# A decoder of four layers on one Trainium2 core: head sums through DRAM by batch, and the output projection inside the score steps

## The reference, cut to what matters

```
q, k, v   = projections of layernorm(x) and of the context (or of x)
num[b,h]  = exp(q k^T / sqrt(8) - rowmax) v          # 8 values per head and query
den[b,h]  = sum of the same exp over the keys
attn      = num / den                                 # in the gated one den >= 1e-30, and * sigmoid(xn Wg + bg)
x        += attn Wo + bo
```

## Time and profile before

| | us |
|---|---|
| time, median of 3 runs (1762.51 to 1765.19) | 1764.23 |
| the profiled execution, its own time | 1759.35 |
| its span, first to last instruction | 1757.6 |
| PE busy over the span | 1491.2 (85%) |
| DVE busy | 1012.8 (58%) |
| ACT busy | 797.9 (45%) |
| POOL busy | 449.6 (26%) |
| mean granted TensorE clock | 0.917 |
| hardware DMA queue, share of 16 engines | 15.3% |

### The profile page before, as it was taken

One profiled execution on the slowest core, in us unless ns is written; L12 is line 12 of the kernel. 1 busy time (PEld: TensorE's weight loads), 2 busy tenths in 40 slices (PEclk: granted clock), 3 DMA queues, 4 the chain that ended last, 5 costly groups with the idle time before them and its releaser, 6 DMA issues. The chain is left out here.

```text
span 1757.6 us, 30799 instructions
## 1 busy us (share of the span) xinstructions
PE 1491.2 (85%) x10804; PEld 754.0 (43%) x10823; DVE 1012.8 (58%) x1950; ACT 797.9 (45%) x1407; POOL 449.6 (26%) x652
## 2 busy tenths in 40 slices
PE   7998999999659999579767899989648888788798
PEld 5777534444424445247433532222305333433266
DVE  5665598883452222546547478994564674467234
ACT  3554447677223333116330237778243564366334
POOL 6121300000234442410235220000023452255200
PEclk9999999999979999689887899999858899999888
DMA  2000542120200000001000163120002421431000
GB/s 94 1 0 0 152 160 84 41 54 1 116 0 0 1 0 0 0 19 36 5 6 1 59 195 121 50 53 15 14 0 83 152 65 29 149 95 54 15 1 24
DMA packets 82104, 85.63 MB, mean 49 GB/s; under 512 B 7085, under 2 KB 67757, under 8 KB 81613
## 3 DMA queue, kind: packets, MB, share of 16 engines
q1 hardware_dynamic: 82008, 84.40, 15.3%
HBM read 51.28 MB, written 32.51 MB: 48 GB/s over the span
## 5 line engine op out<-in xcount | busy, mean ns | idle before, releaser
L1282 ACT ACTIVATE arena<-ps 128x1024 f32<-128x1024 f32 x256 | 262.1, 1024 | 111.9 <-PE ps L1191 111.1
L1176 PE MATMUL ps<-k_stack,q_stack 49*128 49x512 bf16 x512 | 192.5, 387 | 15.2 <-DVE small L1306 13.0
L1191 PE MATMUL ps<-q_stack,k_stack 51*128 51x256 bf16 x1024 | 191.6, 275 | 0.5 <-ACT arena L1282 0.4
L1303 DVE CUSTOM_DVE_ANT_0 small<-ps,mask_b 128x512 bf16<-128x512 f32 x256 | 168.1, 689 | 33.7 <-PE ps L1176 32.1
L1306 DVE TENSOR_REDUCE small<-ps 128x1 f32<-128x512 f32 x256 | 162.2, 685 | 22.5 <-PE ps L1176 21.4
L1492 DVE TENSOR_REDUCE small<-ps 128x6 f32<-128x768 f32 x128 | 122.6, 958 | 76.3 <-PE ps L1374 74.6
L1203 PE MATMUL ps<-arena,v_pad 128*32 128x256 f32 x2048 | 163.7, 394 | 1.1 <-ACT arena L1282 1.1
L1468 ACT ACTIVATE arena<-ps 128x384 f32<-128x384 f32 x256 | 117.8, 488 | 72.9 <-PE ps L1393 72.0
L1076 POOL TENSOR_SCALAR_AFFINE_SELECT arena<-arena 128x256 f32<-128x256 f32 x256 | 102.3, 408 | 80.7 <-ACT arena L1468 80.4
L2543 DVE TENSOR_TENSOR arena<-ps,arena 128x512 f32<-128x512 f32 x64 | 44.3, 692 | 120.9 <-PE ps L2509 120.9
L2558 POOL TENSOR_TENSOR arena<-arena 128x512 f32<-128x512 f32 x64 | 81.1, 1267 | 108.8 <-DVE arena L2543 107.0
(11 more groups left out here) (343 smaller groups left out, 3061.6 us busy)
## 6 DMA issues: line engine op xcount, KB each, us to landing
q_stack<-q_scratch SPq DMA_DIRECT2D x128, 96.0 KB
k_stack<-k_scratch SPq DMA_DIRECT2D x64, 192.0 KB
k_scratch<-arena SPq DMA_DIRECT2D x8, 768.0 KB, 3.7
k_stack<-k_scratch SPq DMA_DIRECT2D x64, 96.0 KB
q_scratch<-arena SPq DMA_DIRECT2D x4, 1152.0 KB, 5.5
arena<-in_ctxT SPq DMA_DIRECT2D x8, 512.0 KB, 6.8
k_scratch<-arena SPq DMA_DIRECT2D x8, 512.0 KB, 4.7
k_scratch<-arena SPq DMA_DIRECT2D x16, 256.0 KB, 4.5
```

Of the source, the lines that this page charges most:

```text
L1176: pe.matmul(ps[:, t, :], c.q_stack[par][64 * e:64 * e + ROW_MAX, pr, t * P:(t + 1) * P], c.k_stack[par][64 * e:64 * e + ROW_MAX, pr, :], s ...
L1191: mm = pe.matmul(ps[:, bank, (ch % 2) * S:(ch % 2 + 1) * S], c.k_stack[prv][64 * e:64 * e + ROWS, pr, ch * P:(ch + 1) * P], c.q_stack[prv] ...
L1282: act.activation(buf.probs[i % 8], ps[:, bank:bank + 2, :].rearrange("p a n -> p (a n)"), ACT.Exp, scale=scale).then_inc(g["probs"].sem, 1)
L1303: dve.tensor_tensor_reduce(buf.junk[t], ps[:, t, :], c.mask_b[:, M_X + t * SC:M_X + (t + 1) * SC], 1.0, FLOOR, op0=ALU.add, op1=ALU.max, a ...
```

## The change

`combine` is gone. A new class `Outputs` does its work batch by batch through two DRAM tensors, inside the steps: batch s-2's sums are stored, loaded back in a layout of 128 partitions (feature d of head q on row 16 d + q), den is inverted as 128 x 32, stored again and loaded eight times, 16 rows each (`spread`); a step later the quotient is made (POOL in wide, DVE in short), projected by PE at i = 7 in bank 7 and added. For batch 7 den itself is loaded eight times and inverted as 128 x 256. All the new DMAs are on SP. The gate's projection and sigmoid move to the end of `project`, before its `keep_clock`. The steps 2 and 3 leave the loop and are written out. The rows of Wo and the columns of Wg follow the new order of features, and the matrices that `combine` used leave the constants.

```diff
+    c.sum_scratch = nc.dram_tensor("sum_scratch", [B, DH + 1, H, S], F32).ap()
+    c.inv_scratch = nc.dram_tensor("inv_scratch", [B, H, S], F32).ap()
...
 def project(...):   # PE, after the last unit
+            if gated:
+                for t in TS:
+                    if t < 2:
+                        pe.wait_ge(g["ln_scaled"].sem, g["ln_scaled"].at(4))
+                    else:
+                        pe.wait_ge(g["gate_out"].sem, g["gate_out"].at(t - 1))
+                    pe.matmul(ps[:, 2 + t % 2, :], w[:, W_G:W_G + P], norm.tile(c.xn, t), start=True, stop=True)\
+                      .then_inc(g["gate_in"].sem, 1)
...                  # ACT, after its last unit
+                for t in TS:
+                    act.wait_ge(g["gate_in"].sem, g["gate_in"].at(t + 1))
+                    act.activation(norm.tile(c.xn, t), ps[:, 2 + t % 2, :], ACT.Sigmoid, bias=w[:, W_BG:W_BG + 1])\
+                       .then_inc(g["gate_out"].sem, 1)
...
+class Outputs:
+    def store_sums(self, buf, sp, b):
+        for i in range(2):
+            sp.wait_ge(g[f"summed_out{i}"].sem, g[f"summed_out{i}"].at(2 * b + 2))
+        for j in range(4):
+            sp.dma_start(c.sum_scratch[b, :, GROUPS * j:GROUPS * j + GROUPS, :],
+                         buf.summed[32 * j:32 * j + DH + 1, :, b * S:(b + 1) * S]).then_inc(g["sums_stored"].sem, 16)
+    def spread(self, sp, out, src, sem):
+        for d in range(DH):
+            sp.dma_start(out[H * d:H * d + H, :], src).then_inc(sem, 16)
+    def load_sums(self, sp, b, last=False):
+        sp.wait_ge(g["sums_stored"].sem, g["sums_stored"].at(64 * (b + 1)))
+        if b > 1:
+            sp.wait_ge(g["quotient"].sem, g["quotient"].at(b - 1))
+        sp.dma_start(self.num[b % 2], c.sum_scratch[b, 0:DH, :, :].rearrange("d q n -> (d q) n")).then_inc(sem, 16)
+        if last:
+            self.spread(sp, self.rec[b % 2], c.sum_scratch[b, DH, :, :], sem)
+        else:
+            sp.dma_start(self.den[b % 2], c.sum_scratch[b, DH, :, :].rearrange("q (a n) -> (q a) n", a=P // H)).then_inc(sem, 16)
+    def spread_inverse(self, sp, b):
+        sp.wait_ge(g["inverted"].sem, g["inverted"].at(b + 1))
+        sp.dma_start(c.inv_scratch[b, :, :].rearrange("q (a n) -> (q a) n", a=P // H), self.den[b % 2]).then_inc(g["inv_stored"].sem, 16)
+        sp.wait_ge(g["inv_stored"].sem, g["inv_stored"].at(16 * (b + 1)))
+        self.spread(sp, self.rec[b % 2], c.inv_scratch[b, :, :], g[f"inv_spread{b % 2}"].sem)
+    def invert(self, dve, par, half, b):      # DVE, 128 x 32, waits for sums_back; guard adds a clamp
+    def divide(self, eng, par, half, ...):    # num * rec, 128 x 256, waits for inv_spread
+    def gate(self, pool, par, b):             # POOL, quot * c.xn
+    def project(self, pe, par, b, bank):      # PE, 128 x 256 fp32
+    def add(self, dve, b, bank):              # DVE, xT += out + bias
...
 def attend_transfers(c, buf, outs, sp, nk, key_mask):
     for s in range(B + 1):
         if 2 <= s < B:
             load(s, 1)
         if s:
             place(s - 1, 1)
+        if s > 1:
+            outs.store_sums(buf, sp, s - 2)
         if s in (1, 2):
             store_parts(...)
         if 1 <= s < B - 1:
             load(s + 1, 0)
+        if s > 1:
+            outs.load_sums(sp, s - 2)
         if s < B:
             place(s, 0)
+        if s > 1:
+            outs.spread_inverse(sp, s - 2)
+    outs.store_sums(buf, sp, B - 1)
+    outs.load_sums(sp, B - 1, True)
...
 attend_wide:  POOL divides batch s-3 at the step's start and adds it to xT at its end
               PE  `if late and i == 7: project_late(...)`  (late: s >= 3)
               ACT `if late and i == 7:` copies the projection (with bias) out of bank 7
               DVE `if n == 22 and s > 1: outs.invert(dve, par, s // 2 - 1, s - 2)`
 attend_short: PE  the same; DVE divides batch s-3 after pair 2, adds it after pair 3,
               and `if before and pr == 5: outs.invert(dve, par, it - 1, s - 2)`
               POOL gates batch s-3 at i == 4 (gated one only)
 both:         sum_waits: the second sum group waits until bank 7 has been read
-    combine(c, slot, **how)
```

More of the change, by code:

```diff
@@ L124 @@
 C_IDENT, C_EPS = 0, P
[L125 to L128, removed]
+C_HEAD = C_EPS + 1
+C_MAGIC = C_HEAD + 2 * P
 C_HSUM = C_MAGIC + 1
@@ L1058, in attend_pool, with step @@
     pool.wait_ge(g["cleared"].sem, g["cleared"].at(1))
-    def step(it, par, front, back, before):
+    def step(it, par, front, back, before, late):
         s = it * 2 + par
@@ L1063, in step @@
             attend_split(c, buf, pool, s - 1, 1, 1 - par)
+        if late and not causal:
+            outs.divide(pool, 1 - par, it - 2 + par)
         for i in range(H):
@@ L1076, in step @@
                 pool.affine_select(diag, diag, [[0, 2], [1, P]], ALU.is_ge, 0.0, 0, -1).then_inc(g["masked"].sem, 1)
+            if late and outs.gated and i == 4:
+                outs.gate(pool, 1 - par, s - 3)
             if front and i == (9 if causal else 0):
                 attend_split(c, buf, pool, s, 0, par)
+        if late and not causal:
+            pool.wait_ge(g["out_kept"].sem, g["out_kept"].at(s - 2))
+            xb = c.xT[:, bass.ds((s - 3) * S, S)]
+            pool.tensor_tensor(xb, xb, outs.kept[1 - par], ALU.add).then_inc(g["residual"].sem, 1)
     attend_steps(c.nc, ENG.Pool, step, causal)
+    if outs.gated:
+        for b in (B - 2, B - 1):
+            outs.gate(pool, b % 2, b)
 def turned_max(c, hf):
@@ L1283, in step @@
                                        scale=scale).then_inc(g["probs"].sem, 1)
+                    if late and i == 7:
+                        act.wait_ge(g["out_proj"].sem, g["out_proj"].at(s - 2))
+                        act.activation(outs.kept[1 - par], ps[:, 7, 0:S], ACT.Identity, bias=outs.w[:, W_BO:W_BO + 1])\
+                           .then_inc(g["out_kept"].sem, 1)
                     if before and i in (1, 5):
```

251 lines of the change are left out of this document (124 added, 127 removed).

## The result

After takes 1834.09 us (median of 4 runs, 1825.56 to 1843.77), before 1763.37 beside it: a ratio of 1.0407, 95% interval 1.0360 to 1.0454. The forecast was 1828, slower.

The account below looks back on a forecast made before the run. PE bounds masked wide steps, DVE unmasked; SP's ordered queue would pace the new short steps. +1.7 + 2.6 + (26.4 - 1.3) + (41.9 - 10.5 + 3.1) = +64 on 1759.35, plus 4.9 to the median: 1828; 8 in 10: 1800 to 1864.

Parts of the forecast that it names:

- wide steps, layer 0 and layer 2: Wide attentions' steps 3 to 8: added projection on PE 2.7 us, inversion on DVE 1.7, half counted where masked.
- wide ends: Behind the wide attentions' last step: batch 7's DRAM chain of 13.3 us replaces `combine`'s 15.1, gaining 1.8 each.
- short steps, self and cross: Layer 3's steps: SP's issues and waits make cycles of 16.5 and 19.4 us against 12.67 and 12.76; +26.4, +41.9.
- short ends: Layer 3 from step 8's start to the last addition: 27.4 us against 28.7 in self, 28.6 against 39.1 in cross.
- ahead of the steps, self and cross: Layer 3's cross projection: added gate work and `keep_clock` run to 1521.7, where SP ended at 1518.6: +3.1 us.
- SP reaches that placement at 8: Short self-attention: maxima turned about 3.3 us after i = 8 at 4.8, so PE's own waits aren't longer.
- Rival B: Short steps: only SP's issue time counts, landings being covered; cycles 13.6 and 16.2, +22 us, 1786; chance 0.10.
- Rival A: Not slower: small DMAs issue cheaply and landings overlap, at 0.05 us each the short steps lose nothing; 1737; chance 0.05.
- C: Rival: landings of 2.5, some slower issues, half clock in the chain, DVE's wait in layer 2; +39, 1867; chance 0.23.
- PE's waits at L1355 ended by DMAs: Sign of being right in layer 3: PE's waits there ended by DMAs of stacks or maxima.
- that leaves 2.9 us to land, so 0: Wide steps: DVE's inversion waits 0 for loaded sums, up to 0.7 us a step if they queue behind the half stack.
- landings of 1.7: A DMA's way after its issue, taken as 1.7 us between two placements' 1.3 and 2.1; bounds 1.3 and 2.5.

Follow-up runs that it names:

- e10: e9 with the inverse spread by eight DMAs, as in after, instead of one: 1822.88 us, ratio 1.0346 to before.
- e6: e5 with the short attentions' new work half a step later on DVE, POOL and PE, same SP queue: 1828.14 us, ratio 1.0327 to before.
- e5: After with each spread as one DMA and step 2's stores of k parts moved behind the placement: 1783.48 us, ratio 1.0086 to before.
- e9: e6 with SP's queue reordered in the short attentions, inverse stored after the next step's second load and placement: 1773.36 us, ratio 1.0083 to before.
- e2: After with each spread as sixteen DMAs of 8 rows instead of eight of 16: 1862.36 us, ratio 1.0601 to before.
- e4: After with step 2's stores of k parts moved behind the placement: 1810.99 us, ratio 1.0302 to before.
- e7: Before with only the gate's projection and sigmoid moved into `project`: 1764.49 us, ratio 0.9985 to before.
- e8: e7 with the new work in the two wide attentions only, with both edits of e5: 1759.19 us, ratio 0.9958 to before.
- e11: e9 with the key mask's rows loaded for batches 0 and 1 only in layer 3's cross-attention, changing its output: 1775.70 us, ratio 1.0102 to before.

## Why the prediction was right, and where its terms were not

| term | forecast | after |
|---|---|---|
| wide steps, layer 0 and layer 2 | +3.5, +4.4 | +10.3, +13.6 |
| wide ends | -1.8 each | -2.5, -2.2 |
| short steps, self and cross | +26.4, +41.9 | +21.8, +33.6 |
| short ends | -1.3, -10.5 | -2.0, -10.7 |
| ahead of the steps, self and cross | 0, +3.1 | -3.0, +7.1 |

**The short steps: the mechanism was right in the main, and its sizes 21 and 25% large.** First new step 20.2 and 21.7 us (forecast 19.9 and 21.5; 1407.29 to 1427.46, 1598.90 to 1620.61), the next four 15.8 and 18.0 (forecast 16.5 and 19.4):

```profile
1598.90 0.31 SPq L975 DMA_DIRECT2D q_stack<-q_scratch  x1
...
1620.61 0.34 SPq L975 DMA_DIRECT2D q_stack<-q_scratch  x1
...
1692.59 0.35 SPq L975 DMA_DIRECT2D q_stack<-q_scratch  x1
```

A DMA in a run of its own kind takes 0.45 (3.58 / 8) or, for the stores, 0.36 (1.45 / 4), not 0.49: 0.8 us a cycle. The stored inverse was back 1.1 after its issue in five of the seven steps of the self-attention (2.2 to 2.3 in the others), not 1.7. The waits in the cycle shown make 2.7 us for a forecast of 2.9, but not by the same parts: 1.3 of them are for the maxima, which the forecast put at nothing ("SP reaches that placement at 8"), and the landings are shorter. So here too part of the agreement is luck. In e10, which has after's issues, the cycle is 16.6. Rival B (issue time only, 1786) named the right resource and left out the waits. e6 shows what one is worth when nothing covers it, 45 us over e5 with the same DMAs, and e9 that an order hides it. Rival A falls with e2 and e10. Of C, DVE's wait came, in another place, and the granted clock fell as well (0.88 and 0.86 over four steps).

What the forecast did not have at all in a short step is DVE in order behind the sums. These are waits of DVE and PE in the cross-attention of after, 1599 to 1709 us:

```profile
DVE small L1073 <- DMA small<-sum_scratch: 13.0, 5, 5.6
...
PE ps L1535 <- DVE small L1675: 12.0, 6, 5.2
```

So "PE's waits at L1355 ended by DMAs", the sign that I had named, came only in part: 4.3 us there were for placed maxima, 12.0 for DVE. That this wait did not set the pace is argued from e10: there DVE waits 1.0 us for sums in 80 us (1600 to 1680; after has 7.5 from 1620 to 1700), and yet the cycle is 18.3 us for 18.0.

**The wide steps: "that leaves 2.9 us to land, so 0".** This is the step that failed. It held for the ordinary step: in 1120 to 1220 us DVE waits 1.5 us in all for sums. But it was read from such a step, and step 2 has three big stores in front of the loads (in the text I named them for the short attentions only). The spacing from step 2 to step 3 grew by 5.7 us in layer 0 and 7.2 in layer 2, the ordinary ones by 0.8 and 1.1, and with e4 the five spacings get 5.4 and 7.4 back. What is left is the steps' own price, in after 0.8 and 1.1 for a forecast of 0.58 and 0.73 (a sixth of 3.5 and 4.4), in e4 0.7 and 0.9. Two groups of after (columns as in the earlier trace rows):

```profile
L1479 DVE TENSOR_REDUCE small<-ps 128x1 f32<-128x512 f32 x256 | 163.4, 685 | 26.0 <-PE ps L1342 24.4
...
L1075 DVE RECIPROCAL small<-small 128x32 f32<-128x32 f32 x28 | 9.9, 352 | 50.2 <-DMA small<-sum_scratch 49.9
```

The maxima cost what they did. The inversion of 128 x 32 takes 0.352, not an eighth of 1.758: (1758 - 352) / 224 = 6.3 ns a column and 0.15 us fixed. The idle time of 49.9 us on its row is not all loss: 13.7 of it is the wait in step 8 of layer 2 alone, where DVE has nothing else.

**The ends.** The last kept sums and the last additions of after, timelines of ACT and DVE (answers to the earlier trace rows):

```profile
1260.28 0.38 ACT L1430 ACTIVATE arena<-ps 128x256 f32<-128x256 f32 x1 [1.78 <-PE ps L1369]
...
1273.10 0.48 DVE L1103 SCALAR_TENSOR_TENSOR xT<-ps,att_w,xT 128x256 f32<-128x256 f32 x1 [1.32 <-PE ps L1095]
...
1531.27 0.48 DVE L1103 SCALAR_TENSOR_TENSOR xT<-ps,att_w,xT 128x256 f32<-128x256 f32 x1 [1.31 <-PE ps L1095]
...
1737.05 0.48 DVE L1103 SCALAR_TENSOR_TENSOR xT<-ps,att_w,xT 128x256 f32<-128x256 f32 x1 [2.12 <-PE ps L1095]
```

12.9 us in layer 2 for 13.3; 26.7 and 28.4 from step 8's start (1505.09, 1709.1) for 27.4 and 28.6. Each within 0.7 us. The landings of 1.7 were right for the chain as a sum: in layer 0 the stored sums are back after 1.9 and the loads after 1.2 (3.1 for 3.4).

**The gate: +3.1, and +7.1 came.** e7 gives +4.2 for the same edit alone. The other 2.9 lies in the projection ahead of it. The window of after from the stage's start to ACT's last part:

```profile
1532.00:1558.70 26.70, 26.06 (x124) 16.96 (x124) 14.56 (x28) 14.47 (x26) 7.48 (x7) 0.89 0.37 118
```

26.7 us at 0.89, where before has 24.2 to the same part. In the 27 us of the DRAM chain before it (1505 to 1532) PE was busy for 12.4 us, at a clock of 0.54; in the 28.5 us before the same point of before it was busy for 23.2, at 0.94. The first 5 us of the projection, in after and in before:

```profile
1532.00:1537.00 5.00, 4.92 (x6) 2.18 (x7) 1.38 (x2) 2.53 (x4) 0.00 (x0) 0.50 0.79 243
...
1488.50:1493.50 5.00, 4.64 (x17) 2.70 (x18) 2.89 (x5) 3.81 (x7) 0.00 (x0) 1.00 0.73 209
```

e7, with the old combination ahead, has 1.00 there and 24.4 us in all. That the idle chain lowered the clock is an inference from these rows; no run held PE busy through it.

**Outside the attentions** +10.6, of which 6.1 in the first 186 us, where the code is the same (the constants are 225 KB for 271). A window of after:

```profile
10.00:20.00 10.00, 9.11 (x48) 9.00 (x48) 3.17 (x8) 3.05 (x7) 5.15 (x4) 0.61 0.33 139
```

The clock there is 0.61, where the profiled execution of before has 1.00. e8 has 0.61 too and needs 188.2 us for that stretch, and is the fastest of all; and e9's kernel, profiled twice, has 0.74 and 1.00 there and needs 182.2 and 177.9 us. So it can come with the execution alone, whatever the change. (The medians lie 70.7 us apart, not 76.2.) The forecast's 64 stands against 65.6, but by luck: 16 us too little in the wide steps, 13 too much in the short ones.

**The page on issue.** Rows of after, by tensor, with KB each and median us to landing:

```profile
arena<-sum_scratch SPq DMA_DIRECT2D x16, 128.0 KB, 2.1
xn<-inv_scratch SPq DMA_DIRECT2D x112, 16.0 KB, 1.7
inv_scratch<-small SPq DMA_DIRECT2D x28, 16.0 KB, 1.5
```

The Trainium skill (DMA: Bandwidth & Descriptors, section Issuing engines are not separate DMA queues) has the sequencer's time to initiate a DMA as usually small relative to the DMA itself. The trace disagrees for small DMAs: 0.45 us of issue stands beside 1.7 to landing, and by e2 and e10 the issues of one queue set the pace of a step. The same page's fixed cost near 2.0 us (section Anatomy of one DMA) is for GpSimd's path; on SP's the trace shows 1.5 to 1.7 for these 16 KB, and 2.4 for the load of den in pieces of 128 B. The prediction's "about 8 higher" with 2.0 does not fit its own range, where 0.4 less makes -16: 0.3 more would be +11 or 12.

**What stays open.** How much of a short step's excess is the granted clock: over four steps of the self-attention it is 0.88 in after and 1.00 in e9, but it is low in the kernels in which PE waits, and no kernel held it up while the waits stood. Whether the late work can be placed so that e11's remaining waits go was not tried, nor whether a second engine's queue could take some of SP's issues. And all the kernels with the new code in the self-attention start its steps 56.6 to 57.4 us into the stage, before, e7 and e8 59.0 to 59.8; the projection there takes 25.0 us at a clock of 0.94 in after and 26.9 at 0.85 in before, and why is not shown.

## What to carry to other kernels

Count the DMAs a loop issues on one queue and multiply by the issue time that your trace shows (0.45 us here) before counting bytes: when the sum nears the loop's cycle, one DMA with a repeated source is worth eight. Then read what each waiting instruction has behind it on its own engine, in every step that differs from the ordinary one, since moving a wait off one in-order engine (e6) only puts it on the next, until that queue's order is changed as well (e9).

## What the runs showed of the hardware that I had not expected

- One DMA whose source is repeated eight times writes 128 partitions in 0.65 us of issue, against 3.58 for eight; halving each of the eight made it 6.49.
- An inversion on DVE has a fixed part of about 0.15 us, from 0.352 at 32 columns and 1.758 at 256.
- The granted clock in the first stretch differs between executions of one kernel: 0.74 and 1.00 from 10 to 20 us in the two profiles of e9's kernel, whose first stretch takes 182.2 and 177.9 us.
